# A CIN tower fed from a scratch array of embedding rows: the scratch array is laid out by chunk in place of by feature

## The reference

```
e  = stack(tbl_f[ids[:, f]])                      # [1024, 32, 64]
x1 = relu(einsum('bhd,bmd,ohm->bod', e,  e, W1) + b1)            # o = 128
x2 = relu(einsum('bhd,bmd,ohm->bod', x1[:, :64], e, W2) + b2)    # o = 128
z  = sum over d of concat(x1[:, 64:], x2)                        # [1024, 192]
h  = relu(concat(z, dense_ctx) @ W_top1 + b_top1)                # 512
h  = relu(h @ W_top2 + b_top2)                                   # 256
y  = h @ W_top3                                                  # [1024, 1]
```

## Time and profile before

| what | value |
|---|---|
| median of 3 runs | 2058.44 us (2058.43 to 2058.59) |
| the profiled execution's own time | 2057.63 us |
| its span, first to last instruction | 2055.8 us |
| PE busy | 2012.2 us, 98% |
| DVE busy | 1983.9 us, 96% |
| ACT, POOL busy | 1631.9 and 1524.0 us, 79% and 74% |
| share of the 16 DMA engines' time in packets of SP's queue | 66.7% |

### The profile page before, as it was taken

The page is one execution under the profiler, slowest core; times in us unless marked ns, Lnnn a source line. Parts: engine busy times, 40 slices in busy tenths (PEclk is TensorE's granted clock), DMA queues, the critical chain, the costliest instruction groups (busy, mean ns, idle before and its releaser), DMA issues.

```text
span 2055.8 us, 28705 instructions
## 1 busy us (share of the span) xinstructions
PE 2012.2 (98%) x6890; PEld 1299.2 (63%) x6890; DVE 1983.9 (96%) x545; ACT 1631.9 (79%) x4755; POOL 1524.0 (74%) x580
## 2 busy tenths in 40 slices
PE   3899999999999999999999999999999999999999
PEld 1566666666666666666666666666666666666664
DVE  5999999999999999999999999999999999999992
ACT  2788788788888888887887887887887888888873
POOL 3877787787787787787787788778778777778520
PEclk9999999999999999999999999999999999999999
DMA  6777777776776776776776776776777777767740
GB/s 185 215 210 208 198 213 203 198 217 199 200 214 200 204 215 196 207 216 190 211 213 195 208 216 192 210 212 191 215 208 197 211 205 201 212 200 206 210 108 1
DMA packets 239331, 406.51 MB, mean 198 GB/s; under 512 B 33377, under 2 KB 50273, under 8 KB 239090
## 3 DMA queue, kind: packets, MB, share of 16 engines
q1 hardware_dynamic: 231026, 397.10, 66.7%
q0 software_dynamic: 8192, 8.40, 2.0%
HBM read 321.49 MB, written 16.78 MB: 165 GB/s over the span
## 4 chain that ended last, share of the span: by engine, by line
DVE 59%; issue 35%; PE 3%; DMA 1%; SPq 1%; ACT 0%; DVEq 0%; POOL 0%; ACTq 0%; POOLq 0%
DVE pnear L459 27%; DVE pfar L459 16%; DVE plo L464 16%; PE acc L521 0%; ACT phi L655 0%; PE acc L527 0%; PE acc L538 0%; PE x1p L586 0%; PE acc L586 0%; PE acc L528 0%; DMA near<-emb_rows 0%; POOL gathered L237 0%; DMA rem_b<-emb_rows 0%; SPq L301 0%; PE acc L592 0%
## 5 line engine op out<-in xcount | busy, mean ns | idle before, releaser
L237 POOL DMA_INDIRECT gathered<-in_tables,idx x256 | 762.0, 2977 | 104.8 <-issue 52.8
L258 POOL TENSOR_TENSOR prod<-near,h 128x2048 f32<-128x2048 f32 x126 | 577.2, 4581 | 174.4 <-PE acc L522 168.7
L655 ACT CAST phi<-pnear 128x4096 fp32r<-128x4096 f32 x128 | 465.9, 3640 | 269.9 <-DVE pnear L459 269.9
L527 PE MATMUL acc<-phi,w2lo 128*128 128x512 f32 x1536 | 603.9, 393 | 14.3 <-ACT phi L655 14.3
L528 PE MATMUL acc<-phi,w2hi 128*128 128x512 f32 x1536 | 603.1, 393 | 0.0
L602 ACT ACTIVATE acc<-acc,bias 128x64 f32<-128x64 f32 (+1 forms) x2048 | 574.9, 283 | 11.7 <-PE acc L528 8.5
L464 DVE TENSOR_TENSOR plo<-pnear,phi 128x4096 fp32r<-128x4096 f32 x128 | 571.8, 4467 | 2.0 <-ACT phi L655 2.0
L459 DVE TENSOR_TENSOR pfar<-far,x1p 128x4096 f32<-128x4096 f32 x128 | 565.8, 4420 | 6.9 <-PE acc L538 1.1
L459 DVE TENSOR_TENSOR pnear<-near,x1p 128x4096 f32<-128x4096 f32 x128 | 564.9, 4414 | 4.7 <-ACT x1p L638 4.7
L521 PE MATMUL acc<-prod,w1T 128*128 128x512 f32 x1024 | 462.5, 594 | 14.3 <-DVE prod L444 12.9
L538 PE MATMUL acc<-pfar,w2T 128*128 128x512 f32 x1024 | 460.3, 592 | 0.0
(11 more groups left out here) (68 smaller groups left out, 535.5 us busy)
## 6 DMA issues: line engine op xcount, KB each, us to landing
near<-emb_rows SPq DMA_DIRECT2D x512, 256.0 KB
far<-emb_rows SPq DMA_DIRECT2D x512, 256.0 KB, 4.2
x1rep<-x SPq DMA_DIRECT2D x256, 256.0 KB, 4.2
h<-emb_rows SPq DMA_DIRECT2D x128, 256.0 KB
emb_rows<-gathered SPq DMA_DIRECT2D x128, 128.0 KB, 3.5
gathered<-in_tables,idx POOLq DMA_INDIRECT x256, 4.9
rem_a<-emb_rows SPq DMA_DIRECT2D x64, 64.0 KB, 3.6
rem_b<-emb_rows SPq DMA_DIRECT2D x64, 64.0 KB, 3.0
```

Source lines behind the costliest of these rows:

```text
L237: nc.gpsimd.indirect_dma_start(out=gathered[s][:, g, :], out_offset=None, in_=a["tables"], in_offset=bass.IndirectOffsetOnAxis(ap=idx[s][: ...
L258: nc.gpsimd.tensor_tensor(prod1[:, :, :], near[(u + 2) % 3][:, :, :], h0[odd][:, :].unsqueeze(1).to_broadcast([P, K1, N]), ALU.mult).then_ ...
L527: nc.tensor.matmul(acc2[s][:, :], w2lo[:, t, :], phi[:, t, :], start=(t == 0), stop=False)
L655: nc.scalar.copy(phi[:, 0:T_NEAR, :], pnear[:, :, :, :].rearrange("p a k n -> p (a k) n")).then_inc(hi_near_ready, 1)
```

## The change

`emb` becomes [CHUNKS, 2 * F * N]: chunk after chunk, each with its 64 rows of 2 KB one behind the other. Parts and places change roles: part k on partition (i, q) now holds feature i + 4q + k, so that the four parts of a partition are four rows that lie together, and near and far are one transfer each, of 8 KB runs. LOADS and the counts of far_in fall accordingly, and `diagonals` swaps its two steps. The store's access to `emb` now has the two chunks of the pair outermost, then 64 runs of 1 KB. The order of the look-ups over the partitions follows (chunk of the pair, feature, place): the offsets of the tables are loaded in two halves, and the ids are cast by DVE in two halves.

```
@@ -20,10 +20,11 @@
 BT = B // P
 GS = P // F
 PAIR_GATHERS = 2 * CB // GS
-ROW = B * D + 1024
 SH = P // F
+CHUNK = 2 * F * N
 HALF = F // 2
 REM = 2 * HALF
+
 
 
 K1 = HALF // SH
@@ -54,7 +55,7 @@
         def sem(name):
             return ctx.enter_context(nc.semaphore(name))
 
-        emb = nc.dram_tensor("emb_rows", [2 * F, ROW], fp32, kind="Internal")
+        emb = nc.dram_tensor("emb_rows", [CHUNKS, CHUNK], fp32, kind="Internal")
 
         ids_n = sb("ids_n", [PAIRS, GS, PAIR_GATHERS, F], i32)
         ids_f = sb("ids_f", [PAIRS, PAIR_GATHERS, F * GS])
@@ -174,14 +175,14 @@
 
         GATHERS = 16 * PAIR_GATHERS
         STORES = 16 * 2
-        LOADS = 16 * (1 + K1)
+        LOADS = 16 * 2
         SMALL_DMAS = 3
         TOP_DMAS = 7
 
         def diagonals(wide, shift, row0=0):
 
             base = wide[:, 64 * row0 + shift:64 * row0 + shift + 1]
-            return bass.AP(base.tensor, base.offset, [list(base.ap[0]), [SH, K1], [65, F], [1, SH]])
+            return bass.AP(base.tensor, base.offset, [list(base.ap[0]), [1, K1], [65, F], [SH, SH]])
 
         def in_tiles(staged):
             return staged.rearrange("o (k i q) -> o k i q", k=K1, i=F)
@@ -282,27 +283,28 @@
         def _(sp):
             sp.dma_start(ids_n[:, :, :, :], a["ids"].rearrange("(r q g) f -> r q g f", q=GS, g=PAIR_GATHERS)
                          ).then_inc(ids_in, 16)
-            sp.dma_start(table_row[:, :], a["table_rows"]).then_inc(ids_in, 16)
+
+            for half in range(2):
+                sp.dma_start(table_row[half * P // 2:(half + 1) * P // 2, :],
+                             a["table_rows"].rearrange("(f half q) one -> half f q one", half=2, q=SH // 2)[half]).then_inc(ids_in, 16)
             sp.dma_start(w1n, a["L0_rec_W1"]).then_inc(w1_in, 16)
             sp.dma_start(w2n, a["L0_rec_W2"]).then_inc(w2_in, 16)
             sp.dma_start(bias1[:, :], a["L0_rec_b1"].rearrange("(p one) -> p one", one=1)).then_inc(small_in, 16)
             sp.dma_start(bias2[:, :], a["L0_rec_b2"].rearrange("(p one) -> p one", one=1)).then_inc(small_in, 16)
             sp.dma_start(dense_n[:, :, :], a["dense_ctx"].rearrange("(t p) c -> p t c", p=P)).then_inc(small_in, 16)
 
-            def load_near(col, s2, s3):
-                sp.dma_start(h0[s2][:, :], bass.AP(emb, col, [[ROW, F], [0, SH], [1, N]])).then_inc(near_in[s3], 16)
-                for k in range(K1):
-                    src = bass.AP(emb, SH * k * ROW + col, [[ROW, F], [ROW, SH], [1, N]])
-                    sp.dma_start(near[s3][:, k, :], src).then_inc(near_in[s3], 16)
-
-            def load_far(col, s):
-                for k in range(K2):
-                    src = bass.AP(emb, SH * (K1 + k) * ROW + col, [[ROW, F], [ROW, SH], [1, N]])
-                    sp.dma_start(far[s][:, k, :], src).then_inc(far_in[s], 16)
-
-            def load_rem(col):
+            def load_near(c, s2, s3):
+                sp.dma_start(h0[s2][:, :], bass.AP(emb, c * CHUNK, [[N, F], [0, SH], [1, N]])).then_inc(near_in[s3], 16)
+                sp.dma_start(near[s3][:, :, :].rearrange("p k n -> p (k n)"),
+                             bass.AP(emb, c * CHUNK, [[N, F], [SH * N, SH], [1, K1 * N]])).then_inc(near_in[s3], 16)
+
+            def load_far(c, s):
+                sp.dma_start(far[s][:, :, :].rearrange("p k n -> p (k n)"),
+                             bass.AP(emb, c * CHUNK + HALF * N, [[N, F], [SH * N, SH], [1, K2 * N]])).then_inc(far_in[s], 16)
+
+            def load_rem(c):
                 for t, f0 in ((rem_a, 0), (rem_b, HALF)):
-                    src = bass.AP(emb, f0 * ROW + col, [[ROW, HALF], [N, 2], [1, N]])
+                    src = bass.AP(emb, c * CHUNK + f0 * N, [[N, HALF], [CHUNK, 2], [1, N]])
                     sp.dma_start(t[:, :], src).then_inc(rem_in, 16)
 
             def replicate_x1():
@@ -314,7 +316,7 @@
                 sp.wait_ge(rows_gathered[s], GATHERS * fills)
                 sp.sem_inc(stores_begun, 1)
                 for f0 in (0, F):
-                    dst = bass.AP(emb, f0 * ROW + pair * (2 * N), [[ROW, F], [PAIR_GATHERS * D, GS], [1, PAIR_GATHERS * D]])
+                    dst = bass.AP(emb, pair * (2 * CHUNK) + f0 * N, [[CHUNK, 2], [PAIR_GATHERS * D, P // 2], [1, PAIR_GATHERS * D]])
                     sp.dma_start(dst, gathered[s][:, :, :]).then_inc(emb_stored, 16)
 
             store_rows(0, 0, 1)
@@ -322,20 +324,20 @@
             load_rem(0)
             load_near(0, 0, 0)
             load_far(0, 0)
-            load_near(N, 1, 1)
+            load_near(1, 1, 1)
             store_rows(1, 1, 1)
             sp.wait_ge(x1_ready, 1)
             replicate_x1()
 
             sp.wait_ge(w2_wide, 1)
             sp.wait_ge(w2_second, 1)
-            load_far(N, 1)
+            load_far(1, 1)
             sp.wait_ge(emb_stored, 2 * STORES)
             sp.wait_ge(rem_prod_ready, 1)
-            load_rem(2 * N)
+            load_rem(2)
             sp.wait_ge(tp_copied, 2)
             sp.wait_ge(p1_ready, 1)
-            load_near(2 * N, 0, 2)
+            load_near(2, 0, 2)
 
             sp.wait_ge(top_zero, 1)
             sp.dma_start(wt1a[0:DENSE, :], a["W_top1"][2 * O - H:2 * O - H + DENSE, :]).then_inc(top_in, 16)
@@ -359,15 +361,15 @@
 
                     sp.wait_ge(emb_stored, STORES * pair + 3 * STORES)
                     sp.wait_ge(rem_prod_ready, pair + 2)
-                    load_rem((c + 3) * N)
+                    load_rem(c + 3)
                 if within(at, 3):
 
                     sp.wait_ge(pnear_ready, c + 1)
                     sp.wait_ge(p1_ready, c + 2)
-                    load_near((c + 3) * N, 1 - odd, u % 3)
+                    load_near(c + 3, 1 - odd, u % 3)
                 if within(at, 2):
                     sp.wait_ge(pfar_ready, c + 1)
-                    load_far((c + 2) * N, odd)
+                    load_far(c + 2, odd)
                 if not odd and within(at, 5):
                     store_rows(pair + 2, (u // 2 + 2) % 3, turn + (u // 2 + 2) // 3 + 1)
 
@@ -379,9 +381,12 @@
 
         @block.vector
         def _(dve):
-            dve.wait_ge(ids_in, 32)
-            nc.vector.tensor_copy(ids_f[:, :, :].rearrange("r g (f q) -> r g f q", q=GS),
-                                  ids_n[:, :, :, :].rearrange("r q g f -> r g f q")).then_inc(ids_float, 1)
+            dve.wait_ge(ids_in, 48)
+            for half in range(2):
+                last = nc.vector.tensor_copy(
+                    ids_f[:, :, half * P // 2:(half + 1) * P // 2].rearrange("r g (f q) -> r g f q", f=F),
+                    ids_n[:, half * GS // 2:(half + 1) * GS // 2, :, :].rearrange("r q g f -> r g f q"))
+            last.then_inc(ids_float, 1)
             dve.wait_ge(ids_turned, 1)
             nc.vector.tensor_scalar(idx_all[:, :, :], tp[0][:, 0:PAIR_GATHERS * PAIRS].rearrange(
                 "p (g r) -> p g r", g=PAIR_GATHERS), table_row[:, :], None, ALU.add).then_inc(idx_all_ready, 1)
@@ -471,7 +476,7 @@
                 if begun(at):
                     dve.wait_ge(lo_near_ready, c)
                 products2(pnear[:, :, :, :], near[u % 3][:, :, :], odd, K1).then_inc(pnear_ready, 1)
-                dve.wait_ge(far_in[odd], 16 * K2 * (turn * (U // 2)) + 16 * K2 * (u // 2 + 1))
+                dve.wait_ge(far_in[odd], 16 * (turn * (U // 2)) + 16 * (u // 2 + 1))
                 if begun(at):
                     dve.wait_ge(lo_far_ready, c)
                     dve.wait_ge(far_used, c)
```

## The result

The changed kernel takes 2097.57 us (median of 6 runs, 2096.14 to 2100.1), the kernel before 2057.89 us (6 runs): ratio 1.0197, interval 1.0184 to 1.021. It is slower by 40 us, where 2059 was forecast, between 2051.5 and 2063.5.

The account below looks back on a forecast made before the run. The prediction took PE, gapless in the loop at 15.355 us a chunk, as the bound. It added 0.5 us for the start and 0 for the loop to 2057.63, plus 0.8 for the median: 2059 us, range 2051.5 to 2063.5.

Parts of the forecast that it names:

- Two engines for the stores: Stores of a pair: outer count of 2 puts them on 2 DMA engines, 6.4 us instead of 0.8, +5.6 where waited for.
- the 0.7 us for the offsets: Start: loading offsets and casting ids in two halves delays the first store by 0.7 us, to 17.5.
- The loop ... Rem goes from 21.52 to 22.6, rem_prod from 26.35 to 27.4 ... All hidden. Cost 0.: Loop: the slower store makes rem and rem_prod later, but nobody waits, so PE stays at 15.355 us a chunk; cost 0.
- The start, +0.5 forecast: Before PE's gapless run: layer1 of chunk 2 moves from 62.95 by +0 to +1 us, taken as +0.5.
- the loads behind x1rep: Start: second rem issued at 45.1, landing at 50.4; near of chunk 2 landing at 52.6 to 53.2 against 52.9.
- far's single issue: Start, SP's queue: far of chunk 1 takes 0.65 us instead of 3.96, a 3.3 us gain eaten by the store.
- the rival with 16 engines: Stores stay on 16 engines, so layer1 of chunk 2 begins 5.6 us earlier: 2052.8, faster by 0.27%; chance 0.20.
- The rival of a later start: Start: stores at 15 GB/s an engine, or slower block loads, add +3.5 to +5 us: 2062 to 2064; chance 0.12.
- the likeliest case: Whole kernel: stores on two engines, first landing 8 us after issue, loop cost hidden; 2056.5 to 2062, chance 0.62.
- The two engines are too slow for the loop: Loop: x1rep late behind a store under 14 GB/s an engine, PE stands still; 2160 at 12 GB/s; chance 0.06.

Follow-up runs that it names:

- e3: The changed kernel, slow stores kept, with POOL's rem_prod moved behind the look-ups and a wait for DVE's far plo: 2064.17 us, ratio 1.0028.
- e2: The kernel before, with rem issued behind near instead of ahead of it in SP's loop: 2103.11 us, ratio 1.0224.
- e1: The changed kernel with each store of a pair cut into one transfer per chunk, on 16 engines: 2057.41 us, ratio 0.9998 to the kernel before.
- e6: e1 with rem of chunk 2 issued ahead of x1rep and far of chunk 1 in the start: 2058.87 us, ratio 1.0007 to the kernel before.

## Why the prediction was wrong

**Right.** PE as the pace of the loop before. Two engines for the stores, and 8.1 us from the first store's issue to its landing, forecast 8. The places that follow came out within 1.6 us: rem at 24.42 (forecast 26.0), prod1 of chunk 0 at 32.54 (near forecast to land at 33.2), x1rep at 41.67 (42.6) and the second rem at 44.82 (45.1). Some of this is luck, for two errors offset each other. The first store went out at 16.35, against 16.81 before and 17.5 forecast, so the 0.7 us for the offsets did not show in this execution; and near took 8.1 us from rem's issue, where 7.2 was taken. By the Trainium skill (DMA: Bandwidth & Descriptors, section "Why a DMA increments its semaphore by 16 and not by 1") the stores had to run on two engines, and the packet counts agree with it in full.

**The step that failed: "The loop ... Rem goes from 21.52 to 22.6, rem_prod from 26.35 to 27.4 ... All hidden. Cost 0."** The loop cost 35 us. Two things were wrong in the step. The shift in the pair shown was 3.3 us and not 1.1 (rem 5.0 us behind x1rep in place of 1.6), and 2.6 on average. And I asked only who waits for rem_prod, and not what runs beside it. The next plo in that timeline begins at 1026.89, half a microsecond after rem_prod, and was stretched by 0.6 us as it was, so 1.1 us more would have put rem_prod inside it. I had the earlier trace rows before me, where rem_parts took 5.26 us, beside a plo of 6.28 (55.45 to 61.73), and took that for a given duration. e3 and e2 show it from both sides: late without a meeting costs nothing in the loop, a meeting without the change costs it all.

**The price.** A full meeting stretches plo by 1.07 us, and DVE had 0.16 us a chunk to spare, which would give (1.07 - 0.31)/2 = 0.38 us a chunk. Measured from 200 to 2000 us, the mean between two pnear is 15.65 us against 15.355, 0.29. Nearly every pair meets, but not all in full: with the mean stretch of 0.87 us a pair the sum is (0.87 - 0.31)/2 = 0.28. 0.29 x 120 = 35 us, and 3.7 of the start, are 38.7 of the 39.3 in the spans. The prediction had read DVE's idle time, 0.05 us a chunk, at its start (0.16 is what DVE has when it runs without a wait), and did not hold a longer DVE instruction against it: that is the term that it put at nothing.

**The start, +0.5 forecast, +3.7 measured.** The mis-sized term is the loads behind x1rep: rem landed 8.2 us after its issue and not 5.3 (44.82 to 53.03), near of chunk 2 at 56.6 and not at 52.9. I had credited far's single issue with 3.3 us of SP's time. But far went out at 43.06 where it began at 39.86 before, its bytes ahead of rem are the same, and e1 shows that the credit was worth nothing even with fast stores. The same mistake is in the rival with 16 engines: 2052.8 forecast, 2057.4 measured. The rival of a later start has nearly the size, +3.5 to +5, but by slower stores, and the stores were not slower than the likeliest case had them (8.1 us for the first where 8 was forecast, the second landed by 44.82 where 45.1 was). A chunk's block is 128 KB, and not the 64 KB that this rival names; no sum uses it.

**The rival that names the loop.** "The two engines are too slow for the loop" had the sign, at 0.06, but its mechanism, x1rep late behind the store, did not happen.

## What to carry to other kernels

When a transfer comes late, ask beside what its consumer will then run, not only who waits for it: instructions of POOL and DVE may shut each other out, and an engine with 1% of margin behind the one that sets the pace then becomes the new bound. Read how many DMA engines a transfer gets from its completion packets, and keep a large count outermost on both sides. Where the DMA engines are busy all the time, as in this start, fewer issues gave nothing back.

## What the runs showed of the hardware

POOL and DVE shut each other out in some pairings, and the times are those of a lock, not of a shared rate. In the pair shown above, the near plo began at 1017.12 and ended at 1021.53. rem_prod, begun at 1018.13, ended at 1022.66, 1.13 us after that (alone it takes 1.29), and the far plo, begun at 1021.46, ended at 1024.81, 2.15 us after rem_prod (alone 2.28). In these rows whoever begins first keeps the other out until it is done. In e6 plo began 0.3 us behind prod1, ended 4.3 us after prod1's end, and rem_parts came 1.1 us after that. A copy of 128x4 by POOL took 4.07 us behind a plo in e2, in place of 0.18. Beside pnear and pfar, which read one input (x1p) from PSUM, prod1 kept its 4.6 us (4.67 at most), rem_prod its 1.29 and DVE its 4.42. Plo reads both inputs from SBUF. In the changed kernel's loop all 57 plo that were stretched by over 0.1 us, from 200 to 2000 us, had a tensor operation of POOL beside them.

POOL's look-ups (gather) are shut out by a plo too, but do not hold it off. In e3's loop 56 look-ups began inside a plo; they took 2.2 to 4.5 us in place of about 1, and each ended 0.8 to 0.9 us after that plo. The 56 near plo that began during a look-up, with up to 0.99 us of it still to run, took 4.43 us at most.

The Trainium skill (SBUF — State Buffer, section "SBUF: two separate sides") states this: a DVE operation with two SBUF inputs and a GpSimd operation that reads SBUF take one pair of ports as an exclusive lock for the whole instruction, and the one that starts later is blocked. The rows of tensor operations and of the copy agree, with 1.07 us a full meeting. The prediction did not use it. That the kind of operand decides was not tried apart here: no run moved an input of plo.

A transfer to device memory on two DMA engines ran at 46 to 51 GB/s in the quiet part behind the loads, 23 to 25 GB/s an engine, a little over the 20.6 that the sum used (DMA view of the changed kernel, 1006 to 1014.9 us, 40 equal slices; a share of 1 tenth is about two of 16 engines):

```profile
DMA  9992601314211111111111138989899899786310
GB/s 405 442 368 111 221 37 74 147 32 143 60 46 51 51 46 46 51 51 46 46 51 51 46 74 161 152 133 138 152 272 267 216 226 203 189 258 216 111 64 18
```
